# Destination rows of four blocks fetched from ScalarE's queue instead of by GpSimd's gather, in a graph attention layer

## The chip, the cores and the metric

One core of one Trainium2 chip runs the whole program. The number that counts is the device time of one execution in microseconds (us). The kernel before took 764.09 us, the median of 3 runs (762.74 to 765.07).

## The reference

A graph has 50,000 nodes with 64 features (`x`), and 25,000 edges, each with a source `src`, a destination `dst` (sorted), a 64-wide attribute and one of 10 types. With R = 10 relation matrices `Wr`:

```
proj   = x @ Wr                                  for every relation
t, h   = proj[src, type], proj[dst, type]
att    = sum(t * tanh(h + eattr))                per edge
a      = softmax of att over the edges of one destination
h_nb   = sum over edges of x[src] * a            per destination
out    = leaky((x + h_nb) @ W1.T) + leaky((x * h_nb) @ W2.T)
result = layernorm(x + out)                      per node
```

Most nodes have no edge. For them `h_nb` is 0, and the result needs `x` and `W1` alone.

## The kernel before, in words

**Two kinds of work run side by side.** The dense part treats every node as if it had no edge: 49 tiles of 1,024 nodes go through TensorE, ScalarE and VectorE and are stored to `out` in order. The edge part treats the edges as 128 partitions of T = 196 consecutive edges, cut into NS = 25 blocks `s` of 8 columns (the last one has 4). The rows of nodes that do have edges are then scattered over the dense rows of `out`. So no scatter may start before every dense row is stored.

**One loop over steps**, `for s in range(-1, NS + 4)`, stands on every engine, with the same `s`. In step `s` the engines do the relation products of block `s`, the softmax sums of block `s - 1`, the two output products of block `s - 2`, the layer norm of the blocks before that, and three dense tiles 3s+3, 3s+4, 3s+5 (D0, D1, D2), as long as there are any: the last tile, 48, is D0 of step 15. Each engine's program is a fixed order written by hand, and semaphores tie the engines together.

**Moving rows.** `xsd` is a ring of RX = 13 blocks; for each of the 8 columns of a block it holds 128 source rows (side 0) and 128 destination rows (side 1).

- POOL (GpSimd) runs one long queue: in `gather` one indirect DMA for each column and side, 384 in all, then in `scatter` one for each column, 196, with one extra gather (`es_end`) and one extra scatter at the end. Between the gathers and the scatters it waits for `o_stored`, that is for the last dense tile to have landed in `out`. `pace` makes POOL wait now and then for a mark of TensorE's progress, chosen by the number of moves made so far, so that it does not run far ahead.
- SP (SyncE) issues the plain loads and stores. It already fetches the last destination column of each of the 8 blocks in `ROW_BLOCKS` row by row (`rows_at`): it loads 8 row numbers from `row_ids` into registers and issues 8 DMAs of 256 bytes, up to six times in a step. These columns are left out of `columns(s)`, which is what `gather` walks. Before the loop, `load_ids(k)` brings the row numbers of those columns into `row_ids` by two DMAs each; VectorE multiplies them by the row size in step 0 (L1120).
- ScalarE (ACT) issues no DMA. Its program in a step is: `tanh`, `dense_copy(D0)`, `heads`, `dense_norm` of an older tile (`o_t`, eight activations), `dense_relu(D0)`, `weights` (waits for VectorE's `delta`), `weigh`, `dense_square`, `final_out`, `pair_copy` (`uwT`), `weigh`, `pair_copy`, `roots` (with two table loads), then in turn `pair_out` (`l`), `dense_copy` (`dT`), `dense_norm` (`o_t`), `dense_square` (`sqd`), `final_square` (`sqf`) and `dense_relu` (`rd`) for D1 and D2.

**Stores of the dense tiles.** In step `s` SP stores tile 2 of step `s - 2` and tiles 0 and 1 of step `s - 1` at fixed places between its row fetches: `load_typ`, `load_e`, `rows_at` (1), store, `load_x`, `rows_at` (2), `load_x`, `rows_at` (3), two stores, three more `rows_at`, `store_hist`. Tile 48 is therefore stored in step 16, behind the third `rows_at`.

Of the kernel before, what the change touches and what calls it, by code (L numbers as in the profile page):

```python
# [40 lines left out]
def gnn_resnorm(nc, x, src, dst, eattr, etype, relw, resw, resw2, out):  # L41
# [14 lines left out]
    def cols(s):  # L56
        return min(COLS, T - s * COLS)
# [24 lines left out]
    CHUNK = 8  # L82
    PER_STEP = 6

    def columns(s):
        return [(j, side) for side in range(2) for j in range(cols(s)) if not (s in ROW_BLOCKS and (j, side) == (cols(s) - 1, 1))]

# [8 lines left out]
    with ExitStack() as ctx:  # L96
# [38 lines left out]
        fix_i = sb("fix_i", [P, 2], I32)  # L135
        row_ids = sb("row_ids", [1, len(ROW_BLOCKS), P], I32)

# [51 lines left out]
        gathered = sems("gathered", RX)  # L189
        rows_in, ids_in = sems("rows_in", len(ROW_BLOCKS)), sem("ids_in")  # L190
        at_done = sem("at_done")
        typ_in = sems("typ_in", RT)
# [33 lines left out]
        def pe_marks():  # L226
# [56 lines left out]
            return marks, ends  # L283

        block = ctx.enter_context(nc.Block())

        @block.sync
        def _(sp):
# [64 lines left out]

            x_bytes = x.rearrange("n f -> (n f)").bitcast(U8)
            ROW = D * 4

            def load_ids(k):
                c = ROW_BLOCKS[k] * COLS + cols(ROW_BLOCKS[k]) - 1
                every = dst[0:(P - 1) * T].rearrange("(p c) -> c p", c=T)
                sp.dma_start(row_ids[0:1, k, 0:P - 1], every[c:c + 1, :], allow_slow_non_contiguous=True).then_inc(ids_in, DMA)  # L360
                last = (P - 1) * T + c if c < LASTC else c - LASTC
                sp.dma_start(row_ids[0:1, k, P - 1:P], dst[last:last + 1].rearrange("(a c) -> a c", a=1)).then_inc(ids_in, DMA)
# [26 lines left out]
            load_e(1)  # L389
            for k in range(len(ROW_BLOCKS)):  # L390
                load_ids(k)

# [97 lines left out]
        def _(pe):  # L490
# [12 lines left out]
            def turn_in(s):  # L503
                pe.wait_ge(gathered[s % RX], sum(len(columns(n)) for n in range(s % RX, s + 1, RX)) * DMA)
                if s in ROW_BLOCKS:
                    pe.wait_ge(rows_in[ROW_BLOCKS.index(s)], P * DMA)
                wait(pe, masked, s * R)
                half = cols(s) // 2
                for j in range(cols(s)):
                    k = j % 2 * half + j // 2  # L510
                    mm = pe.transpose(xT_ps[:, k * P:(k + 1) * P], xsd[:, s % RX, j, :, :].rearrange("p a f -> p (a f)"),
                                      ident[:, :])
                mm.then_inc(xT_done, 1)
# [147 lines left out]
        def _(act):  # L661
# [76 lines left out]
            def final_out(f, s):  # L738
# [5 lines left out]
                ins.then_inc(fmul_done, 1)  # L744

            act.wait_ge(setup_m, 2)
            for s in range(-1, LAST + 1):
# [9 lines left out]
                if D0 is not None:  # L757
                    dense_copy(D0)
                if 0 <= f < NS:
                    for g in range(groups(f)):  # L760
                        heads(f, g)
                for n in tiles(s - 2)[2:3]:
                    dense_norm(n)
                if D0 is not None:
                    dense_relu(D0)
                if 0 <= e < NS:
                    weights(e)
                    weigh(e, 0)
# [16 lines left out]
                for n in done[0:1]:  # L785
                    dense_norm(n)
                if quarters > 1:
                    pair_out(f, 1)
                if D0 is not None:
                    dense_square(D0)  # L790
                if 0 <= l < NS:
                    final_square(l)
                if D1 is not None:
                    dense_relu(D1)
                if quarters > 2:
                    pair_out(f, 2)
                if D2 is not None:
                    dense_copy(D2)
                for n in done[1:2]:
                    dense_norm(n)  # L800
                if quarters > 3:
                    pair_out(f, 3)
                if D1 is not None:
                    dense_square(D1)
                if s == NS + 1:

                    act.wait_ge(fx_v, 7)
                    act.activation(before[:, :], off[:, :], ACT.Exp, bias=fix[:, 5:6]).then_inc(fx_act, 1)
                    act.activation(fix[:, 6:7], fix[:, 2:3], ACT.Exp, bias=fix[:, 5:6]).then_inc(fx_act, 1)
# [18 lines left out]
        def _(v):  # L828
# [213 lines left out]
            for s in range(-1, LAST + 1):  # L1042
# [74 lines left out]
                if s == 0:  # L1117

                    v.wait_ge(ids_in, 2 * len(ROW_BLOCKS) * DMA)
                    v.tensor_scalar(row_ids[:, :, :], row_ids[:, :, :], float(4 * D), None, ALU.mult).then_inc(at_done, 1)  # L1120
# [92 lines left out]
```

## Time and profile before

| | us |
|---|---|
| median of 3 runs | 764.09 |
| span of the profiled execution (its own time; the page gives no more) | 764.9 |
| POOL busy | 581.8 (76%) |
| VectorE busy | 634.8 (83%) |
| PE busy | 556.2 (73%) |
| ScalarE busy | 499.1 (65%) |

A busy share counts only the instructions themselves. POOL shows 76%, but its digits in the slices of the span are 7 from the second slice to the last but one and never fall: each of its DMAs is followed by a short stretch called issue in which nothing is waited for. VectorE's digits are 9 until slice 34 and near 0 behind it; the last eighth of the span is scatters. The DMA engines are busy 40% or less of the time nearly everywhere.

### The profile page before, as it was taken

What the parts mean: (1) busy time and instruction counts of PE and PEld (TensorE: products, weight loads), DVE (VectorE), ACT (ScalarE), POOL (GpSimd) and SP (SyncE); (2) the same over time, 40 slices, a digit from 0 to 9 for tenths busy, and PEclk for the clock granted to TensorE, in tenths of its full rate; (3) what the DMA queues carried; (4) which work ended last, traced back from release to release, by engine and by line L of the source; (5) the groups of instructions that cost most, each with busy time, mean ns of one, the idle gap of its engine ahead of it and who ended that gap; (6) DMA issues with size and microseconds to landing.
All of it is one profiled execution on the core that took longest, in us unless ns stands there. A gap on an engine that the chain in (4) does not pass through costs nothing. (4 is left out here: it accounts for less than half of the span.)

```text
span 764.9 us, 14665 instructions
## 1 busy us (share of the span) xinstructions
PE 556.2 (73%) x3780; PEld 293.9 (38%) x3780; DVE 634.8 (83%) x1115; ACT 499.1 (65%) x1474; POOL 581.8 (76%) x590
## 2 busy tenths in 40 slices
PE   1887888888789788888889887788888788632000
PEld 0652454445345345345345343333333333321000
DVE  1689999999999999999999999999999899742010
ACT  0366677679778779779778777765656446755040
POOL 6777777777777777777777777777777777777776
PEclk9999999999999999999999999999999999755555
DMA  5463435434434434434444332422112221000000
GB/s 134 105 191 81 124 89 144 124 87 145 124 95 137 125 106 126 133 106 117 138 107 115 104 104 73 108 73 75 48 46 74 75 83 44 28 26 17 19 18 16
DMA packets 49457, 70.41 MB, mean 92 GB/s; under 512 B 17450, under 2 KB 20966, under 8 KB 49374
## 3 DMA queue, kind: packets, MB, share of 16 engines
q1 hardware_dynamic: 30750, 52.33, 21.2%
q0 software_dynamic: 18624, 17.16, 10.9%
q8 instruction: 30, 0.49, 0.3%
q14 instruction: 53, 0.43, 0.2%
HBM read 45.61 MB, written 25.78 MB: 93 GB/s over the span
## 5 line engine op out<-in xcount | busy, mean ns | idle before, releaser
L441 POOL DMA_INDIRECT xsd<-in_x,ends_i x384 | 378.2, 985 | 118.0 <-issue 108.6
L543 PE MATMUL t_ps<-xm,w_rel 64*64 64x512 f32 (+1 forms) x1000 | 270.3, 622 | 39.7 <-DVE xm L912 39.2
L912 DVE SCALAR_TENSOR_TENSOR xm<-typ,xT_ps 128x1024 f32<-128x1024 f32 (+1 forms) x250 | 292.4, 1187 | 2.6 <-issue 2.6
L545 PE MATMUL h_ps<-xm,w_rel 64*64 64x512 f32 (+1 forms) x1000 | 270.2, 622 | 0.0
L465 POOL DMA_INDIRECT out<-out_r,row_i x196 | 200.6, 1023 | 59.7 <-issue 55.5
L560 PE MATMUL y_ps<-bd_cat,dT 128*128 128x256 f32 x392 | 97.9, 394 | 17.6 <-DVE zd L974 14.8
L691 ACT ACTIVATE o_t<-zd,rstd 128x64 f32<-128x64 f32 x392 | 98.8, 337 | 14.9 <-DVE rstd L996 14.9
L543 PEld LDWEIGHTS t_ps<-xm,w_rel 64*64 64x64 f32 x1000 | 52.7, 135 | 142.7 <-DVE xm L912 117.4
L578 PE MATMUL s_ps<-bd_both,uwT 128*128 128x128 f32 x392 | 73.4, 313 | 36.6 <-issue 35.9
L578 PEld LDWEIGHTS s_ps<-bd_both,uwT 128*128 128x128 f32 x392 | 54.9, 203 | 115.1 <-issue 95.3
L560 PEld LDWEIGHTS y_ps<-bd_cat,dT 128*128 128x128 f32 x392 | 72.5, 195 | 30.9 <-issue 12.8
L954 DVE SCALAR_TENSOR_TENSOR es<-es,wd,wx 128x64 f32<-128x64 f32 x196 | 55.7, 284 | 11.7 <-ACT wx L704 0.6
L698 ACT ACTIVATE wd<-delta 128x16 f32<-128x16 f32 (+1 forms) x25 | 5.4, 216 | 88.7 <-DVE delta L942 84.4
L568 PE MATMUL tr_ps<-ident,uw 128*128 128x128 f32 x196 | 34.4, 302 | 27.0 <-ACT uwT L718 15.6
L723 ACT COPY l<-s_ps 128x256 f32<-128x256 f32 x98 | 35.2, 359 | 26.9 <-PE s_ps L578 26.9
L545 PEld LDWEIGHTS h_ps<-xm,w_rel 64*64 64x64 f32 x1000 | 52.7, 135 | 0.0
L704 ACT ACTIVATE wx<-xsd,wd 128x64 f32<-128x64 f32 x196 | 52.1, 337 | 0.8
L711 ACT ACTIVATE h_t<-es,rs 128x64 f32<-128x64 f32 x196 | 49.4, 337 | 0.0
L743 ACT ACTIVATE out_r<-zcf,rstd 128x64 f32<-128x64 f32 x196 | 49.2, 333 | 0.1
L568 PEld LDWEIGHTS tr_ps<-ident,uw 128*128 128x128 f32 x196 | 22.3, 150 | 66.8 <-issue 35.0
L974 DVE TENSOR_TENSOR zd<-rd,y_ps 128x512 f32<-128x512 f32 x49 | 33.4, 682 | 9.2 <-ACT rd L677 9.2
L684 ACT ACTIVATE sqd<-zd 128x512 f32<-128x512 f32 x49 | 30.9, 631 | 12.7 <-DVE zd L984 12.6
(143 smaller groups left out, 742.1 us busy)
## 6 DMA issues: line engine op xcount, KB each, us to landing
xsd<-in_x SPq DMA_DIRECT2D x1024, 0.2 KB
x_in<-in_x SPq DMA_DIRECT2D x48, 256.0 KB
typ<-typ_d SPq DMA_DIRECT2D x24, 512.0 KB
out<-o_t SPq DMA_DIRECT2D x48, 256.0 KB
xsd<-in_x,ends_i POOLq DMA_INDIRECT x384
hist<-es SPq DMA_DIRECT2D x24, 256.0 KB, 2.0
ea<-in_edge_attr SPq DMA_DIRECT2D x24, 224.0 KB
out<-out_r,row_i POOLq DMA_INDIRECT x196, 2.1
```

The lines of the kernel that those rows point to most:

```text
L441: pool.indirect_dma_start(xsd[:, s % RX, j, side, :], None, x[:, :], bass.IndirectOffsetOnAxis(ap=ends_i[:, side, c:c + 1], axis=0),).then ...
L465: pool.indirect_dma_start(out[:, :], bass.IndirectOffsetOnAxis(ap=row_i[:, c:c + 1], axis=0), out_r[:, s % RW, j, :], None, bounds_check=t ...
L543: pe.matmul(t_ps[h * D:(h + 1) * D, 0:n], w_rel[0:D, r, :], xm[0:D, b, h * n:(h + 1) * n], start=(r == 0), stop=(r == R - 1), skip_group_c ...
L545: mm = pe.matmul(h_ps[(1 - h) * D:(2 - h) * D, 0:n], w_rel[D:P, r, :], xm[D:P, b, (1 - h) * n:(2 - h) * n], start=False, stop=(r == R - 1) ...
L560: mm = pe.matmul(y_ps[:, j * 2 * P:(j + 1) * 2 * P], dT[:, d % 2, j * P:(j + 1) * P], bd_cat.rearrange("p k f -> p (k f)"), start=True, st ...
L568: mm = pe.transpose(tr_ps[:, j * P:(j + 1) * P], uw[:, g * QUAD + j, :, :].rearrange("p k f -> p (k f)"), ident[:, :])
L578: mm = pe.matmul(s_ps[:, YQ + j * P:YQ + (j + 1) * P], uwT[:, q // 2, k * P:(k + 1) * P], bd_both[:, :], start=True, stop=True)
L691: ins = act.activation(o_t[:, d % RO, j * D:(j + 1) * D], zd[:, d % RZ, j * D:(j + 1) * D], ACT.Copy, scale=rstd[:, s % 2, d % 3, j:j + 1])
L704: ins = act.activation(wx[:, j, :], xsd[:, e % RX, j, 0, :], ACT.Copy, scale=wd[:, e % 2, 0, j:j + 1])
L711: ins = act.activation(h_t[:, j, :], es[:, f % RS, j, :], ACT.Copy, scale=rs[:, f % 2, j:j + 1])
L912: v.scalar_tensor_tensor(xm[:, (s * R + r) % RM, 0:n], typ[:, s % RT, 0:n], float(r), xT_ps[:, 0:n], ALU.is_equal, ALU.mult).then_inc(mask ...
L954: v.scalar_tensor_tensor(es[:, e % RS, j, :], old, wd[:, e % 2, 1, j:j + 1], wx[:, j, :], ALU.mult, ALU.add).then_inc(chain_done, 1)
```

## The change

Besides the last destination column, the second last one of blocks 8, 13, 18 and 24 is now fetched row by row, from ScalarE's queue. POOL's gather leaves it out, so `columns` of these blocks is one shorter. `fetch(s, place)` stands at twelve places of ScalarE's step and issues two 256-byte DMAs at each, rows in order, from step 1 on until all 4 x 128 rows are out (step 22). Every 32 rows it first loads 32 row numbers into registers. TensorE waits for one more semaphore before it turns such a block. SP loads four more lists of row numbers before the loop. The row sizes and the definition of `x_bytes` only move.

```diff
     ROW_BLOCKS = list(range(5, 25, 3)) + [24]
+    ACT_BLOCKS = [8, 13, 18, 24]
+    ACT_CHUNK, ACT_STEP, ACT_AT_ONCE = 32, 24, 2
+
+    def fetched(s):
+        return [(cols(s) - 1, 1)] * (s in ROW_BLOCKS) + [(cols(s) - 2, 1)] * (s in ACT_BLOCKS)
     def columns(s):
-        return [(j, side) for side in range(2) for j in range(cols(s)) if not (s in ROW_BLOCKS and (j, side) == (cols(s) - 1, 1))]
+        return [(j, side) for side in range(2) for j in range(cols(s)) if (j, side) not in fetched(s)]
...
-            for k in range(len(ROW_BLOCKS)):
-                load_ids(k)
+            for k, b in enumerate(ROW_BLOCKS):
+                load_ids(k, b * COLS + cols(b) - 1)
+            for k, b in enumerate(ACT_BLOCKS):
+                load_ids(len(ROW_BLOCKS) + k, b * COLS + cols(b) - 2)
...
+                if s in ACT_BLOCKS:
+                    pe.wait_ge(act_rows_in[ACT_BLOCKS.index(s)], P * DMA)
...
+            def fetch(s, place):
+                for n in range((s - 1) * ACT_STEP + place * ACT_AT_ONCE, (s - 1) * ACT_STEP + (place + 1) * ACT_AT_ONCE):
+                    k, p = divmod(n, P)
+                    if s < 1 or k >= len(ACT_BLOCKS):
+                        return
+                    b = ACT_BLOCKS[k]
+                    if p == 0:
+                        act.wait_ge(at_done, 1)
+                        wait(act, z2_done, b - RX + 1)
+                    if p % ACT_CHUNK == 0:
+                        for i in range(ACT_CHUNK):
+                            ids[i] = act.alloc_register(f"act_id{n}_{i}")
+                        act.load([ids[i] for i in range(ACT_CHUNK)], row_ids[0:1, len(ROW_BLOCKS) + k, p:p + ACT_CHUNK])
+                    at = act.snap(ids[p % ACT_CHUNK], donate=True, min_val=0, max_val=(N - 1) * ROW)
+                    act.dma_start(xsd[p:p + 1, b % RX, cols(b) - 2, 1, :].bitcast(U8),
+                                  x_bytes[bass.DynSlice(at, ROW)].rearrange("(a c) -> a c", a=1)).then_inc(act_rows_in[k], DMA)
...
                 if quarters > 2:
                     pair_copy(f, 1)
+                fetch(s, 6)
                 if s >= 0:
                     roots(s)
...
-                    v.wait_ge(ids_in, 2 * len(ROW_BLOCKS) * DMA)
+                    v.wait_ge(ids_in, 2 * (len(ROW_BLOCKS) + len(ACT_BLOCKS)) * DMA)
```

ScalarE's order in the middle of a step, before. `uwT` is `pair_copy`, `wx` is `weigh`, `sd` and `fix` with their table loads are `roots`, `l` is `pair_out`:

```order
L718 COPY uwT<-tr_ps 128x512
L704 ACTIVATE wx<-xsd,wd 128x64 x4
L718 COPY uwT<-tr_ps 128x512
L730 ACT_TABLE_LOAD
L730 ACTIVATE sd<-ssq,eps_t 128x32
L731 ACT_TABLE_LOAD
```

The same place in the changed kernel (line numbers are those of the changed file):

```order
L727 COPY uwT<-tr_ps 128x512
L713 ACTIVATE wx<-xsd,wd 128x64 x4
L771 DMA xsd<-in_x 1x256 x2
L727 COPY uwT<-tr_ps 128x512
L771 DMA xsd<-in_x 1x256 x2
L739 ACT_TABLE_LOAD
L739 ACTIVATE sd<-ssq,eps_t 128x32
L740 ACT_TABLE_LOAD
```

Two row fetches (place 5) now stand between the second `wx` group and the second `uwT` copy, and two (place 6) between that copy and the first table load.

ScalarE's order in the last third of a step, before. `sqf` is `final_square`; `rd`, `dT`, `o_t` and `sqd` belong to the dense tiles D1 and D2:

```order
L736 ACTIVATE sqf<-zcf 128x512
L677 ACTIVATE rd<-y_ps 128x512
L723 COPY l<-s_ps 128x256
L672 COPY dT<-tr_ps 128x512
L691 ACTIVATE o_t<-zd,rstd 128x64 x8
L723 COPY l<-s_ps 128x256
L684 ACTIVATE sqd<-zd 128x512
```

The same place in the changed kernel, in a step in which the load of 32 row numbers falls on place 8:

```order
L745 ACTIVATE sqf<-zcf 128x512
L769 TENSOR_LOAD row_ids
L771 DMA xsd<-in_x 1x256 x2
L686 ACTIVATE rd<-y_ps 128x512
L732 COPY l<-s_ps 128x256
L681 COPY dT<-tr_ps 128x512
L771 DMA xsd<-in_x 1x256 x2
L700 ACTIVATE o_t<-zd,rstd 128x64 x8
L771 DMA xsd<-in_x 1x256 x2
L732 COPY l<-s_ps 128x256
L693 ACTIVATE sqd<-zd 128x512
```

The load and place 8 are new ahead of `rd`, place 9 ahead of the `o_t` group, and place 10 behind it.

SP's order at the end of the part ahead of the loop, before (`x_in` are dense tiles 4, 5 and 6):

```order
L360 DMA row_ids<-in_dst 1x127x1
L362 DMA row_ids<-in_dst 1x1
L305 DMA x_in<-in_x 128x512 x3
L330 DMA typ<-typ_d 128x1024
L344 DMA ea<-in_edge_attr 112x512
```

The same place in the changed kernel:

```order
L365 DMA row_ids<-in_dst 1x127x1
L367 DMA row_ids<-in_dst 1x1
L365 DMA row_ids<-in_dst 1x127x1
L367 DMA row_ids<-in_dst 1x1
L365 DMA row_ids<-in_dst 1x127x1
L367 DMA row_ids<-in_dst 1x1
L365 DMA row_ids<-in_dst 1x127x1
L367 DMA row_ids<-in_dst 1x1
L314 DMA x_in<-in_x 128x512 x3
L339 DMA typ<-typ_d 128x1024
L353 DMA ea<-in_edge_attr 112x512
```

Twelve pairs of such loads now stand ahead of the tiles where eight stood; everything behind them moves back by four pairs. On POOL the one row of gathers reads x380 instead of x384, and nothing else moves there.

## Rows read from the trace of the kernel before

**Rows 1.** The page's costliest groups: busy us, mean ns | idle before, releaser.
```profile
L441 POOL DMA_INDIRECT xsd<-in_x,ends_i x384 | 378.2, 985 | 118.0 <-issue 108.6
```
**Rows 2.** The chain that ended last, in order of time: start us, us, what.
```profile
759.15 0.97 POOL out L465
...
760.43 0.97 POOL out L482
```
**Rows 3.** Step 11: us, busy PE, PEld, DVE, ACT, POOL; clock, DMA share, GB/s.
```profile
337.80:366.00 28.20, 23.73 (x168) 13.09 (x164) 27.59 (x47) 22.89 (x70) 21.49 (x23) 1.00 0.41 119
```
**Rows 4.** Timeline of POOL where the gathers end: start us, us, instruction.
```profile
497.59 0.94 POOL L441 DMA_INDIRECT xsd<-in_x,ends_i  x1 [0.30 <-issue]
498.83 1.00 POOL L465 DMA_INDIRECT out<-out_r,row_i  x1 [0.30 <-issue]
```
**Rows 5.** Timeline of SP in steps 15 and 16.
```profile
467.22 3.21 SPq L311 DMA_DIRECT2D out<-o_t  x2
471.54 9.87 SPq L377 DMA_DIRECT2D xsd<-in_x  x24
...
494.35 0.73 SPq L311 DMA_DIRECT2D out<-o_t  x2
```
**Rows 6.** The page's DMA issues: KB each, median us to landing.
```profile
hist<-es SPq DMA_DIRECT2D x24, 256.0 KB, 2.0
```
**Rows 7.** Timeline of ScalarE: the norm of tile 48.
```profile
487.42 2.02 ACT L691 ACTIVATE o_t<-zd,rstd 128x64 f32<-128x64 f32 x8
```
**Rows 8.** SP's own waits: us in total, times, longest us.
```profile
SPq L311 <- ACT o_t L691: 43.6, 18, 4.3
```
**Rows 9.** All instructions on row_ids: ns min/median/max, first and last start us.
```profile
L374 SPq TENSOR_LOAD <-row_ids x128: 697/782/1088, 51.7 to 625.7; - x128
L360 SPq DMA_DIRECT2D row_ids<-in_dst x8: 583/597/702, 18.6 to 31.8; - x8
L362 SPq DMA_DIRECT2D row_ids<-in_dst x8: 937/1109/1982, 19.4 to 32.4; - x8
L1120 DVE TENSOR_SCALAR row_ids<-row_ids x1: 806/806/806, 48.8 to 48.8; 1x1024 int32<-1x1024 int32 x1
```
**Rows 10.** Timeline of SP: the first tiles behind the lists of row numbers.
```profile
33.58 1.30 SPq L305 DMA_DIRECT2D x_in<-in_x  x3
```
**Rows 11.** Timeline of PE in step 0: tile 4 is turned, then relation 6.
```profile
40.35 0.66 PE L553 MATMUL tr_ps<-ident,x_in 128*128 128x128 f32 x4
41.65 0.64 PE L543 MATMUL t_ps<-xm,w_rel 64*64 64x512 f32 x1 [0.64 <-DVE xm L912]
```
**Rows 12.** Timeline of SP: eight row fetches one behind the other.
```profile
302.65 2.60 SPq L377 DMA_DIRECT2D xsd<-in_x  x8
```
**Rows 13.** Timeline of ScalarE in step 10.
```profile
312.11 0.21 ACT L698 ACTIVATE wd<-delta 128x16 f32<-128x16 f32 x1 [2.89 <-DVE delta L942]
...
318.20 0.58 ACT L718 COPY uwT<-tr_ps 128x512 f32<-128x512 f32 x1 [0.30 <-issue]
...
322.85 2.02 ACT L691 ACTIVATE o_t<-zd,rstd 128x64 f32<-128x64 f32 x8 [0.17 <-DVE rstd L996]
...
326.08 0.58 ACT L677 ACTIVATE rd<-y_ps 128x512 f32<-128x512 f32 x1
...
326.88 0.58 ACT L672 COPY dT<-tr_ps 128x512 f32<-128x512 f32 x1
327.36 2.02 ACT L691 ACTIVATE o_t<-zd,rstd 128x64 f32<-128x64 f32 x8
329.29 0.35 ACT L723 COPY l<-s_ps 128x256 f32<-128x256 f32 x1
```
**Rows 14.** Timeline of VectorE in the same step.
```profile
324.41 0.71 DVE L1032 SCALAR_TENSOR_TENSOR zcf<-zs,zf 128x512 f32<-128x512 f32 x1
...
326.76 0.68 DVE L974 TENSOR_TENSOR zd<-rd,y_ps 128x512 f32<-128x512 f32 x1
...
329.79 1.17 DVE L1011 SCALAR_TENSOR_TENSOR l<-l 128x1024 f32<-128x1024 f32 x1
```

More of the change, by code:

```diff
@@ L135, in gnn_resnorm @@
         fix_i = sb("fix_i", [P, 2], I32)
-        row_ids = sb("row_ids", [1, len(ROW_BLOCKS), P], I32)
+        row_ids = sb("row_ids", [1, len(ROW_BLOCKS) + len(ACT_BLOCKS), P], I32)
         xsd = sb("xsd", [P, RX, COLS, 2, D])
@@ L190, in gnn_resnorm @@
         rows_in, ids_in = sems("rows_in", len(ROW_BLOCKS)), sem("ids_in")
+        act_rows_in = sems("act_rows_in", len(ACT_BLOCKS))
         at_done = sem("at_done")
@@ L283, in pe_marks @@
             return marks, ends
+        x_bytes = x.rearrange("n f -> (n f)").bitcast(U8)
+        ROW = D * 4
         block = ctx.enter_context(nc.Block())
@@ L352, in store_hist, with load_ids @@
                              es[:, e % RS, 0:cols(e), :]).then_inc(hist_stored[e % RS], DMA)
[L354 to L358, printed above, removed]
+            def load_ids(k, c):
                 every = dst[0:(P - 1) * T].rearrange("(p c) -> c p", c=T)
@@ L744, in final_out @@
                 ins.then_inc(fmul_done, 1)
+            ids = {}
+            def fetch(s, place):
[14 more added lines that the diff above has]
+                                  x_bytes[bass.DynSlice(at, ROW)].rearrange("(a c) -> a c", a=1)).then_inc(act_rows_in[k], DMA)
             act.wait_ge(setup_m, 2)
@@ L758, in _ @@
                     dense_copy(D0)
+                fetch(s, 0)
                 if 0 <= f < NS:
@@ L761, in _ @@
                         heads(f, g)
+                fetch(s, 1)
                 for n in tiles(s - 2)[2:3]:
                     dense_norm(n)
+                fetch(s, 2)
                 if D0 is not None:
@@ L768, in _ @@
                     weigh(e, 0)
+                fetch(s, 3)
                 if DP is not None:
@@ L772, in _ @@
                     final_out(o - 1, s - 1)
+                fetch(s, 4)
                 if quarters > 0:
@@ L776, in _ @@
                     weigh(e, 1)
+                fetch(s, 5)
                 if quarters > 2:
                     pair_copy(f, 1)
+                fetch(s, 6)
                 if s >= 0:
@@ L786, in _ @@
                     dense_norm(n)
+                fetch(s, 7)
                 if quarters > 1:
@@ L792, in _ @@
                     final_square(l)
+                fetch(s, 8)
                 if D1 is not None:
@@ L798, in _ @@
                     dense_copy(D2)
+                fetch(s, 9)
                 for n in done[1:2]:
                     dense_norm(n)
+                fetch(s, 10)
                 if quarters > 3:
@@ L804, in _ @@
                     dense_square(D1)
+                fetch(s, 11)
                 if s == NS + 1:
```

## The prediction, made before the changed kernel ran

> **What bounds the kernel now.** I read the slices of the page first, then the costliest groups, the chain of waits, the timeline of POOL where it changes from gathers to scatters, and the timeline of SP there. The slices show POOL equally busy from start to end. Its gather takes 0.985 us and stands behind 0.31 us of issue (118.0 / 384) [rows 1], 1.29 us a move, and the chain that ended last is scatters and nothing else [rows 2]. So POOL's queue sets the end, and a gather less is worth up to 1.29 us, if nothing else then holds POOL.
>
> Something stands ready to hold it. Before the first scatter POOL waits until the last dense tile, 48, has landed. The last gather starts at 497.59 and the first scatter at 498.83 [rows 4]. SP issues the two parts of tile 48 from 494.35 to 495.08 [rows 5]; a store of SP's lands 2.0 us after its issue [rows 6], so at 497.1, and with 0.3 us of issue the scatter could start at 497.4. The slack is 498.83 - 497.4 = 1.4 us. POOL may come earlier to this place, but it gets no more than 1.4 us out of it, as long as tile 48 is stored when it is now.
>
> Why is tile 48 stored so late? Its norm on ScalarE runs from 487.42 to 489.44 [rows 7], 4.9 us ahead of the store. SP is the late one: from its two stores of step 15, which end at 470.43 behind a wait for ScalarE, it works with small gaps up to 494.35 [rows 5]. That wait is the usual one: 43.6 us over 18 times, 2.4 us each [rows 8]. So SP follows the dense loop with 2.4 us to spare in a step, and tile 48's store comes a fixed 23.9 us behind the norm of tile 46 in step 15. Whatever delays the loop up to step 15 delays the first scatter by the same amount, less 1.4 us.
>
> The loop itself is bound by VectorE: 27.59 us of 28.20 in step 11, with ScalarE at 22.89 [rows 3]. ScalarE's spare 5.3 us lie mostly where it waits for `delta` (2.89 us at 312.11) [rows 13]. From the second `uwT` copy at 318.20 to the last `l` at 329.29 the rows leave no gap but 0.17 us.
>
> **The change, part by part.**
>
> *POOL.* Four gathers go: 4 x 1.29 = 5.2 us. The gathers then end near 493.3, and the wait for tile 48 is late next. By the slack above 1.4 us of the 5.2 remain, the rest becomes waiting. Pace marks only hold POOL if the loop slips, and by no more than it slips, which is late at the hand-over anyway; scatters further on stand behind results long finished, so no second gain or loss: every us at the hand-over is one at the end.
>
> *SP ahead of the loop.* Four more lists, each 0.60 + 1.11 us and two gaps of 0.05 [rows 9]: 4 x 1.75 = 7.0 us. The loads behind them are queued: tiles 4 to 6, types and edges of the next blocks. Tile 4 is issued by 34.0 (the first of three from 33.58 on [rows 10]) and, at 2.0 us to landing, is there at 36.0; with the change at 43.0. TensorE turns it at 40.35 [rows 11]: 2.65 us late. TensorE's own wait of 0.64 us behind it goes in return [rows 11], which leaves 2.0. TensorE is followed by the tanh and the product at the step's end, so the loop keeps this. Bounds 0 (it is swallowed later) and 2.7; I take 2.0. VectorE's multiplication of `row_ids` at 48.8 grows by half its 0.81 us [rows 9]; the lists are issued by about 40.6, so they are there. It lies in VectorE's wait for the tanh of step 0 and I cost it at nothing; without that cover 0.4.
>
> *ScalarE, the DMAs.* SP needs 0.325 us for each row fetch (2.60 / 8 [rows 12]), 0.65 for a pair, 7.8 for the 24 of a step. The trace shows no DMA on ScalarE. One bound is 0, when ScalarE works on activations handed to it earlier while the pair is issued; the other is all 7.8 exposed. I take cover where a group of eight activations (2.0 us) or a wait stands around the pair: places 0 to 5 (the 2.89 us at `delta` swallow what shows), 7, 8, 10 and 11. Two remain. Place 6 stands behind a copy that waits for TensorE (318.20, 0.58 us long [rows 13]); the pair ends at 318.85 plus the hand-over of the next waits, some 0.3 us late, less the 0.17 us idle ahead of `o_t`. Place 9 stands behind the `dT` copy at 326.88, so that the `o_t` group starts at about 327.6 in place of 327.36 [rows 13]. What waits for it: VectorE's `zd` at 326.76 needs `rd`, done at 326.66, and its `l` at 329.79 needs the copy done at 329.64 [rows 13, 14]: 0.1 and 0.15 us to spare. So about 0.25 us of a step shows on VectorE; over the 14 steps 1 to 14 that is 3.5 us (bounds 0 and, where the six places of that stretch show in full, 6 x 0.65 x 14 = 55).
>
> *ScalarE, the loads of row numbers.* 16 loads of 32 registers; SP's loads of 8 take 0.70 to 1.09 us, median 0.78 [rows 9]. Bounds 0.78 and 4 x 0.78 = 3.1; I take 1.1, nearer the row. With 24 rows in a step they fall on places 0, 4, 8 and none in turn. On 0 and 4 they are covered. On place 8, in steps 3, 7 and 11, the pair and the load take 1.75 us from the end of `zcf` at 325.12 [rows 14] on, which is 326.87, where `rd` started at 326.08: 0.8 late, 0.7 on VectorE, 0.6 beyond what is counted: 3 x 0.6 = 1.8.
>
> *SP beside ScalarE.* If the two queues get in each other's way, SP's last 23.9 us, in which it no longer waits, grow. Bounds 0 and 24 x 0.325 = 7.8; I take 1.0.
>
> *The new waits.* The rows of block 8 are out by step 6 and used at the end of step 7, those of 13, 18 and 24 by steps 11, 16 and 22 for 12, 17 and 23: a step of 28.20 [rows 3] covers the landing. `at_done` and `z2_done` are set by then. Cost nothing; if a block came late, TensorE and all behind it would wait.
>
> *Sum.* The loop slips 2.0 + 3.5 + 1.8 = 7.3 by the hand-over, SP adds 1.0: 8.3. Less 1.4 of slack: +6.9. The span of 764.9 becomes 771.8; the median stood 0.8 below the profiled span, so 771.0.
>
> **A page's rule beside the rows.** The trace shows ScalarE's eight-activation groups but not how far its queue is filled. The Trainium skill, "Advanced Engine Details and Errata", section Engine Queue Depths, gives ScalarE a queue of 8 on trn2: by that a pair issued behind a group of eight is hidden, as I assume. No row here tests it.
>
> **Rivals.**
>
> *All of ScalarE's issue is hidden, the hand-over holds.* For it: 5.3 us idle in a step. Against: the gapless stretch. The loop slips only by the 2.0 of the start, or not at all: 764.1 - 1.4 + 2.0 = 764.7, down to 762.7. No change. This is the case on the other side, not slower: the mechanism is POOL's shorter queue cut off at tile 48's landing, and it decides as soon as the loop and SP slip less than 1.4 + 2.3 = 3.7 us in all.
>
> *POOL gets its 5.2 us.* Only if tile 48 lands earlier or is not waited for; nothing in the rows makes SP earlier. 764.1 - 5.2 = 758.9.
>
> *ScalarE's issue is not hidden.* Its activations stand still while it issues: 22.89 + 7.8 + 0.8 of loads = 31.5 us against 28.20, 3.3 a step, 14 steps: 46, with start and slack about 811. ScalarE is then the bound.
>
> *SP and ScalarE share what issues the fetches.* SP has 2.4 us to spare in a step [rows 8]. If half of ScalarE's 7.8 us went on SP's queue, 1.5 a step would be lost, 21 over 14 steps, and 3.9 in the last stretch: 764.1 - 1.4 + 2.0 + 21 + 3.9 = 789.6. For it: SP is busy nearly without a gap. Against: a fetch is 256 bytes, and the two are often out of phase. The Trainium skill, "Perfetto Trace Analysis", section DMA Instruction — HWDGE, says that the unit which makes descriptors is shared between sequencers and locked while one uses it; by that such waits exist on both queues. The trace has one such queue only and cannot show it.
>
> **Chances.** The forecast, a slip that gives 767 to 782: 0.56. Hidden: 0.19. POOL's 5.2: 0.04. Not hidden: 0.11. Shared unit: 0.10. A difference under 0.3%, 2.3 us, can't be told from none here. Faster by more: 0.04. Within: 0.20, the hidden case and a sliver of the forecast. Slower: 0.76. The range 763.5 to 787 leaves out the fastest case with the lower end of the hidden one and most of the last two.
>
> **What would show it.** In the profile after: POOL's row has x380 gathers and an idle gap ahead of the first scatter, which starts near 506, with tile 48's store at about 503; the steps are 28.5 to 28.9 us long where they were 28.2; TensorE waits near 40 for tile 4. Wrong if the first scatter starts before 498, if the steps keep their length (then ScalarE's issue is free), or if ScalarE has no idle time left (then it is not hidden at all). SP's wait for ScalarE's `o_t` shrinking from 2.4 us each would point to the shared unit.

## The result, and the profile after

The changed kernel takes 782.09 us (median of 4 runs, 781.45 to 782.42); beside it the kernel before took 764.58 us (4 runs, 762.74 to 765.07). The ratio is 1.0226 (95% interval 1.0208 to 1.0243), 17.5 us slower. The forecast was 771.0, 6.9 us more than before: the direction was right, and the time lies in the range of 763.5 to 787.0, but the slip of the loop was more than twice what the sum gave.

The page of the kernel after, costliest groups (busy us, mean ns | idle before, releaser):

```profile
L448 POOL DMA_INDIRECT xsd<-in_x,ends_i x380 | 374.8, 986 | 125.2 <-issue 105.2
L1014 DVE TENSOR_TENSOR zd<-rd,y_ps 128x512 f32<-128x512 f32 x49 | 33.3, 680 | 19.5 <-ACT rd L686 19.4
```

Four gathers went at the old price each [rows 1]. VectorE's `zd` now waits 19.4 us for ScalarE's `rd`, where it waited 9.2 before. The timeline of POOL at the hand-over (start us, us, instruction, idle before it and its releaser):

```profile
501.43 0.94 POOL L448 DMA_INDIRECT xsd<-in_x,ends_i  x1 [0.30 <-issue]
515.75 1.00 POOL L472 DMA_INDIRECT out<-out_r,row_i  x1 [13.37 <-DMA out<-o_t]
```

The timeline of SP in steps 15 and 16:

```profile
482.33 6.36 SPq L320 DMA_DIRECT2D out<-o_t  x2
489.80 9.85 SPq L382 DMA_DIRECT2D xsd<-in_x  x24
...
512.51 0.73 SPq L320 DMA_DIRECT2D out<-o_t  x2
```

The first scatter starts 16.9 us later than before (515.75 against 498.83 [rows 4]) and stands behind 13.4 us of waiting for tile 48. From the end of SP's two stores of step 15 to the store of tile 48 it is 23.8 us, and 23.9 before [rows 5]. So SP's last stretch did not grow. All of the 16.9 us came with the loop.

Where the loop lost them is read from the first `xm` of a block on VectorE, the start of a step, once before and once after. Timeline of VectorE, kernel before, blocks 0, 1, 3, 4, 5 and 16:

```profile
31.81 2.34 DVE L912 SCALAR_TENSOR_TENSOR xm<-typ,xT_ps 128x1024 f32<-128x1024 f32 x2
...
55.50 1.21 DVE L912 SCALAR_TENSOR_TENSOR xm<-typ,xT_ps 128x1024 f32<-128x1024 f32 x1
...
108.89 1.21 DVE L912 SCALAR_TENSOR_TENSOR xm<-typ,xT_ps 128x1024 f32<-128x1024 f32 x1
137.08 1.21 DVE L912 SCALAR_TENSOR_TENSOR xm<-typ,xT_ps 128x1024 f32<-128x1024 f32 x1
165.26 1.21 DVE L912 SCALAR_TENSOR_TENSOR xm<-typ,xT_ps 128x1024 f32<-128x1024 f32 x1
...
473.99 1.21 DVE L912 SCALAR_TENSOR_TENSOR xm<-typ,xT_ps 128x1024 f32<-128x1024 f32 x1
```

The same of the kernel after:

```profile
32.20 1.21 DVE L952 SCALAR_TENSOR_TENSOR xm<-typ,xT_ps 128x1024 f32<-128x1024 f32 x1
...
60.00 1.20 DVE L952 SCALAR_TENSOR_TENSOR xm<-typ,xT_ps 128x1024 f32<-128x1024 f32 x1
...
114.39 1.21 DVE L952 SCALAR_TENSOR_TENSOR xm<-typ,xT_ps 128x1024 f32<-128x1024 f32 x1
145.99 1.21 DVE L952 SCALAR_TENSOR_TENSOR xm<-typ,xT_ps 128x1024 f32<-128x1024 f32 x1
174.23 1.21 DVE L952 SCALAR_TENSOR_TENSOR xm<-typ,xT_ps 128x1024 f32<-128x1024 f32 x1
...
492.24 1.21 DVE L952 SCALAR_TENSOR_TENSOR xm<-typ,xT_ps 128x1024 f32<-128x1024 f32 x1
```

The differences are 0.4, 4.5, 5.5, 8.9, 9.0 and 18.3 us. Step 0 lost 4.1 us, step 3 lost 3.4, step 4 nearly nothing. Over all steps up to block 16, from the same kind of row:

| lost in | us |
|---|---|
| start and step 0 (lists of row numbers) | 0.4 + 4.1 |
| steps 3, 7, 11, 15 (load on place 8) | 3.4 + 2.1 + 2.2 + 3.0 = 10.7 |
| steps 2, 6, 10, 14 (load on place 4) | 1.0 + 0.5 + 0.3 + 0.8 = 2.6 |
| all others (load on place 0, or none) | 0.5 |
| sum | 18.3 |

18.3 less the slack of 1.4 is the 16.9 at the hand-over. Steps with 24 fetches and no load on places 4 or 8 cost next to nothing. A load of 32 row numbers is the first row here, a fetch on ScalarE's and on SP's queue are the others (ns min/median/max):

```profile
L769 ACTq TENSOR_LOAD <-row_ids x16: 2132/2144/2542, 56.3 to 599.4; - x16
...
L771 ACTq DMA_DIRECT2D xsd<-in_x x512: 213/213/537, 58.6 to 628.6; - x171
...
L382 SPq DMA_DIRECT2D xsd<-in_x x1024: 227/228/347, 57.0 to 648.1; - x171
```

The forecast took 1.1 us for the load. It is 2.14. The timeline of ScalarE and VectorE in step 3, kernel after:

```profile
132.83 0.62 ACT L745 ACTIVATE sqf<-zcf 128x512 f32<-128x512 f32 x1
...
134.66 0.75 ACTq L771 DMA_DIRECT2D xsd<-in_x  x2
...
135.51 0.60 ACT L686 ACTIVATE rd<-y_ps 128x512 f32<-128x512 f32 x1 [2.06 <-issue]
...
136.14 0.69 DVE L1014 TENSOR_TENSOR zd<-rd,y_ps 128x512 f32<-128x512 f32 x1 [2.02 <-ACT rd L686]
```

The load ends where the pair begins, so it began at about 132.4. Only `sqf` was left to ScalarE meanwhile. `rd` starts 2.06 us after `sqf` is done, and VectorE, the bound of the loop, stands still for 2.02 of them. Before, the two stood without a gap; this is ScalarE in the same place of the kernel before:

```profile
127.34 0.62 ACT L736 ACTIVATE sqf<-zcf 128x512 f32<-128x512 f32 x1
127.86 0.58 ACT L677 ACTIVATE rd<-y_ps 128x512 f32<-128x512 f32 x1
```

And the start. TensorE turns tile 4 and goes on with a relation (timeline of PE, kernel after):

```profile
44.02 0.66 PE L562 MATMUL tr_ps<-ident,x_in 128*128 128x128 f32 x4 [3.21 <-DMA x_in<-in_x]
44.61 1.09 PE L552 MATMUL t_ps<-xm,w_rel 64*64 64x512 f32 x1
```

It waits 3.2 us for the tile, and the matmuls behind the wait take 1.09 us instead of 0.64 [rows 11]. The granted clock in that stretch is 0.58 (first row, after); before it was 1.00 (second row; us, busy PE, PEld, DVE, ACT, POOL, clock, DMA share, GB/s):

```profile
44.00:48.00 4.00, 3.98 (x16) 1.93 (x17) 2.78 (x3) 3.02 (x10) 3.08 (x4) 0.58 0.90 263
```
```profile
44.00:48.00 4.00, 3.78 (x26) 1.56 (x25) 3.68 (x5) 4.00 (x15) 2.91 (x4) 1.00 0.33 90
```

Of the two levels, 2.4 GHz is 1.00 and 1.2 GHz is 0.50, so a mean of 0.58 is the lower level for most of the stretch. TensorE had been idle for 3.2 us ahead of it.

### The profile page after: what moved, and what is told of

It is laid out like the page before. It is cut to its first block and busy times, and to the rows that moved or that the text cites. A ratio compares the mean times of both kernels' runs of the same rounds, so it can differ in the third digit from the quotient of the medians.

```text
span 780.7 us, 15717 instructions
## 1 busy us (share of the span) xinstructions
PE 560.1 (72%) x3780; PEld 295.0 (38%) x3780; DVE 636.2 (81%) x1115; ACT 502.0 (64%) x1474; POOL 577.4 (74%) x586
## 3 DMA queue, kind: packets, MB, share of 16 engines
q10 hardware_dynamic: 1024, 0.13, 0.1%
## 5 line engine op out<-in xcount | busy, mean ns | idle before, releaser
L552 PE MATMUL t_ps<-xm,w_rel 64*64 64x512 f32 (+1 forms) x1000 | 273.3, 627 | 35.8 <-DVE xm L952 35.1
L554 PE MATMUL h_ps<-xm,w_rel 64*64 64x512 f32 (+1 forms) x1000 | 273.3, 627 | 0.0
L569 PE MATMUL y_ps<-bd_cat,dT 128*128 128x256 f32 x392 | 98.9, 397 | 16.9 <-DVE zd L1014 14.2
L700 ACT ACTIVATE o_t<-zd,rstd 128x64 f32<-128x64 f32 x392 | 98.8, 337 | 14.9 <-DVE rstd L1036 10.4
L994 DVE SCALAR_TENSOR_TENSOR es<-es,wd,wx 128x64 f32<-128x64 f32 x196 | 55.7, 284 | 11.7 <-ACT wx L713 0.6
L1014 DVE TENSOR_TENSOR zd<-rd,y_ps 128x512 f32<-128x512 f32 x49 | 33.3, 680 | 19.5 <-ACT rd L686 19.4
L1051 DVE SCALAR_TENSOR_TENSOR l<-l 128x1024 f32<-128x1024 f32 (+1 forms) x25 | 29.7, 1190 | 13.9 <-ACT l L732 13.7
```

Of the source, the lines that this page charges most:

```text
L552: pe.matmul(t_ps[h * D:(h + 1) * D, 0:n], w_rel[0:D, r, :], xm[0:D, b, h * n:(h + 1) * n], start=(r == 0), stop=(r == R - 1), skip_group_c ...
L554: mm = pe.matmul(h_ps[(1 - h) * D:(2 - h) * D, 0:n], w_rel[D:P, r, :], xm[D:P, b, (1 - h) * n:(2 - h) * n], start=False, stop=(r == R - 1) ...
L569: mm = pe.matmul(y_ps[:, j * 2 * P:(j + 1) * 2 * P], dT[:, d % 2, j * P:(j + 1) * P], bd_cat.rearrange("p k f -> p (k f)"), start=True, st ...
L700: ins = act.activation(o_t[:, d % RO, j * D:(j + 1) * D], zd[:, d % RZ, j * D:(j + 1) * D], ACT.Copy, scale=rstd[:, s % 2, d % 3, j:j + 1])
L994: v.scalar_tensor_tensor(es[:, e % RS, j, :], old, wd[:, e % 2, 1, j:j + 1], wx[:, j, :], ALU.mult, ALU.add).then_inc(chain_done, 1)
```

## The experiments

Theory C: the scatters start when tile 48 has landed, the loop's slip passes through less 1.4 us, and the slip is made of the lists and of loads that stick out of ScalarE's cover. Theory D (and other letters where named): another part carries it. Ratios are to the kernel before, timed on the same chip: 763.81 us for the first four, 764.96 for the next four, 765.21 for the last two.

**1. The gathers gone, nothing in their place.**

```diff
-        return [... if not (s in ROW_BLOCKS and (j, side) == (cols(s) - 1, 1))]
+        left_out = [(cols(s) - 1, 1)] * (s in ROW_BLOCKS) + [(cols(s) - 2, 1)] * (s in [13, 16, 19, 22])
+        return [... if (j, side) not in left_out]
```

> The kernel before with four gathers fewer and nothing in their place: the second last destination column of blocks 13, 16, 19 and 22 is left out, so those blocks compute with the rows that their ring slot held before. Nothing else differs. Theory A (the hand-over from gathers to scatters waits for tile 48's landing): the four gathers are worth 4 x 1.29 = 5.2 us of POOL's queue, but only 1.4 us come through: 764.6 - 1.4 = 763.2, no measurable change, and in the profile an idle gap of about 4 us on POOL ahead of the first scatter that ends with the landing of out<-o_t. Rival B (POOL's queue alone sets the end): 764.6 - 5.2 = 759.4, and no gap.

Measured: 763.58 us, ratio 0.9997 (0.9985 to 1.0009). POOL's waits (us in total, times, longest):

```profile
POOL out L466 <- DMA out<-o_t: 5.3, 1, 5.3
```

Four gathers are worth nothing that can be told while tile 48 is stored where it is: POOL turns them into waiting. That is A. The 1.4 us that A lets through don't show in the time either (0.2 us, and the interval reaches from 1.1 less to 0.7 more).

**2. The same, with the store of tile 48 earlier.** In step 16 it stands ahead of SP's second group of row fetches, where it stood behind the third.

```diff
+                last = tiles(s - 1)[0:1] == [ND - 1]
+                if last:
+                    store_o(ND - 1)
                 rows_at((s - 1) * PER_STEP + 1)
                 load_x(d + 5)
                 rows_at((s - 1) * PER_STEP + 2)
-                for n in tiles(s - 1)[0:2]:
+                for n in [] if last else tiles(s - 1)[0:2]:
```

> As e1_no_fetch (the same four columns are left out), and in step 16 SP issues the store of tile 48 ahead of its second row fetch group instead of behind its third. Its norm is done at 489.4, so the store can go out at 489.5 to 490.2 and land near 492.2, ahead of POOL's last gather (493.3). Theory A: now all of the 5.2 us come through, 759.4, and the gap on POOL is gone. If something else than the landing of tile 48 held POOL in e1_no_fetch, this changes nothing against it.

Measured: 760.69 us, ratio 0.9955 (0.9940 to 0.9970). The first scatter, in the timeline of POOL:

```profile
494.30 1.53 POOL L469 DMA_INDIRECT out<-out_r,row_i  x1 [3.36 <-DMA out<-o_t]
```

It starts 4.5 us earlier than before, and the kernel is 3.1 us faster than the one before, 2.9 faster than experiment 1: the landing of tile 48 sets the end, and SP's place for its store sets the landing. The full 5.2 us did not come through (759.4 was expected), and POOL still waits 3.4 us. Part of this is that the loop of the profiled execution was already 2.2 us late at its first block and 1.2 late at block 16, for a reason that was not looked into.

**3. Only the four lists more.** The kernel before with `load_ids` for twelve columns instead of eight; all 384 gathers stay.

```diff
-            for k in range(len(ROW_BLOCKS)):
-                load_ids(k)
+            for k, b in enumerate(ROW_BLOCKS):
+                load_ids(k, b * COLS + cols(b) - 1)
+            for k, b in enumerate([8, 13, 18, 24]):
+                load_ids(len(ROW_BLOCKS) + k, b * COLS + cols(b) - 2)
```

> The kernel before with four more lists of row numbers ahead of the loop (12 pairs of loads on SP, not 8), which nobody uses; all 384 gathers stay. The changed kernel's step 1 starts 4.1 us later than before, as TensorE waits 3.2 us for tile 4 and then multiplies at half speed for a while. Theory A: step 1 again starts about 4.1 us late, the slip is kept until the hand-over, and of it 4.1 - 1.4 = 2.7 us show in the time: 767.3. Rival: the slip is swallowed by later steps, or POOL does not depend on it: 764.6 within 1 us. My forecast had priced the slip at 2.0, which would give 765.2.

Measured: 766.49 us, ratio 1.0031 (1.0018 to 1.0044), 2.7 us. Timeline of PE, and the granted clock of the stretch behind it (0.59, the third number from the end):

```profile
43.06 0.66 PE L554 MATMUL tr_ps<-ident,x_in 128*128 128x128 f32 x4 [2.67 <-DMA x_in<-in_x]
```
```profile
44.00:48.00 4.00, 4.00 (x16) 2.09 (x8) 2.35 (x3) 2.77 (x10) 2.89 (x4) 0.59 0.95 257
```

The same wait, the same lower clock. The loop is 3.4 us late at block 1 and 2.8 at block 16. That is A.

**4. Only the loads.** The changed kernel, but POOL gathers all 384 columns and ScalarE issues one DMA of 64 bytes behind each load, where the other 31 fetches are left out.

```diff
-        return [(cols(s) - 1, 1)] * (s in ROW_BLOCKS) + [(cols(s) - 2, 1)] * (s in ACT_BLOCKS)
+        return [(cols(s) - 1, 1)] * (s in ROW_BLOCKS)
...
-                    act.dma_start(xsd[p:p + 1, b % RX, cols(b) - 2, 1, :].bitcast(U8),
-                                  x_bytes[bass.DynSlice(at, ROW)]...
+                        act.dma_start(spare[0:1, q, :].bitcast(U8),
+                                      x_bytes[bass.DynSlice(at, 64)]...
```

> The changed kernel without its row fetches on ScalarE: POOL gathers all 384 columns again, ScalarE still makes its 16 loads of 32 registers at the same places and, so that the registers are used, one 64-byte DMA behind each load. The four lists stay. Theory C (the loads, 2.14 us each where I had taken 1.1, are what the forecast missed): step starts slip by 4.1 us at step 0, by about 2.5 us in each of steps 3, 7, 11 and 15, by some 0.5 in steps 2, 6, 10 and 14, nothing elsewhere: 4.1 + 10 + 2 = 16 at the hand-over, less 1.4: 764.6 + 14.6 = 779. Rival D (the fetches themselves take the time, and the loads only happen to stand near): the slip stays near 4.1 + 2 and the time near 769.

Measured: 775.76 us, ratio 1.0165 (1.0141 to 1.0189), 12.0 us. It lies between the two expectations, nearer to C, which had a slip of 16 us at block 16 where it is 12.2. Without the lists of experiment 3 it is 9.3 us for 16 loads. The four steps with a load on place 8 lose 1.8, 1.5, 1.9 and 2.4 us. `rd` in step 3 (timeline of ScalarE):

```profile
133.83 0.60 ACT L687 ACTIVATE rd<-y_ps 128x512 f32<-128x512 f32 x1 [1.73 <-issue]
```

**5. Only the DMAs.** All 512 fetches stand where they are; the row numbers are loaded once, in step 1, and used again, so that the rows fetched are not the right ones.

```diff
-                    if p % ACT_CHUNK == 0:
+                    if n == 0:
```

> The changed kernel with its 512 row fetches at the same places, but with the row numbers loaded once (32 registers in step 1) and used again for all of them: the fetched rows are the wrong ones, the traffic is the same. The loads alone made the loop slip by 8.5 us (e4_loads_only against e3_lists_only), the whole change by 14 beyond the lists. Theory C (the fetches are covered by ScalarE's queued activations and cost only where they stand behind a load that has used the cover up): the slip is that of the lists, 3.4 to 4.1 us, plus at most 2; the time 764.6 + 5 - 1.4 = 768, and the step starts move nowhere by more than 0.5 us. Rival E (loads and fetches add up): slip 4 + 6 = 10, 773.

Measured: 768.69 us, ratio 1.0049 (1.0033 to 1.0065), 3.7 us, of which the lists are 2.7. About 1 us is left for 512 fetches, no more than the intervals. The steps agree: from block 1 to block 16 the loop loses 1.2 us. Timeline of ScalarE at place 8:

```profile
327.54 0.22 ACTq L771 DMA_DIRECT2D xsd<-in_x  x1
327.80 0.62 ACT L745 ACTIVATE sqf<-zcf 128x512 f32<-128x512 f32 x1
327.92 0.22 ACTq L771 DMA_DIRECT2D xsd<-in_x  x1
328.32 0.58 ACT L686 ACTIVATE rd<-y_ps 128x512 f32<-128x512 f32 x1
```

The pair is issued while `sqf` stands handed over behind `sqd` (327.27 to 327.90) and while it runs, and `rd` follows without a gap. ScalarE's DMAs are hidden behind activations already handed over. That is C.

**6. The lists later.** The changed kernel, with the four lists behind tile 7's load in step 0 instead of ahead of the loop.

```diff
-            for k, b in enumerate(ACT_BLOCKS):
-                load_ids(len(ROW_BLOCKS) + k, b * COLS + cols(b) - 2)
...
                 load_x(d + 4)
+                if s == 0:
+                    for k, b in enumerate(ACT_BLOCKS):
+                        load_ids(len(ROW_BLOCKS) + k, b * COLS + cols(b) - 2)
```

> The changed kernel with its four lists of row numbers loaded in step 0, behind the load of tile 7, where they delay no tile that is waited for. Theory A: TensorE no longer waits for tile 4, step 1 starts within 0.5 us of before, and the slip at the hand-over goes from 18.3 to about 14.2: 782.1 - 4.1 = 778. Rival: the later steps swallow it, 782.

Measured: 776.66 us, ratio 1.0152 (1.0121 to 1.0184). It stands 11.7 us above the kernel before, where the changed kernel stands 17.5 above it: 5.8 us less. Block 1 starts 0.3 us ahead of the kernel before, where it stood 4.5 behind; block 16 is 12.4 us late, where it was 18.3.

**7. The loads at place 0.** The changed kernel, with the 24 row numbers of a step loaded at its first place: 22 loads instead of 16, and none on place 4 or 8.

```diff
-                    if p % ACT_CHUNK == 0:
-                        for i in range(ACT_CHUNK):
+                    if n % ACT_STEP == 0:
+                        count = min(ACT_STEP, len(ACT_BLOCKS) * P - n)
+                        for i in range(count):
                             ids[i] = act.alloc_register(f"act_id{n}_{i}")
```

> The changed kernel with 24 row numbers loaded at place 0 of every step (22 loads, about 0.22 + 24 x 0.06 = 1.7 us each) in place of 32 at places 0, 4 and 8 in turn. 22 loads take more of ScalarE's time in all than 16 (37 against 34 us), but place 0 stands ahead of ScalarE's long wait for delta. Theory C (what counts is where a load stands): slip 4.1 from the lists plus at most 2, time near 768; no jump in steps 3, 7, 11 and 15. Rival D (what counts is the time that loads and fetches take on ScalarE's queue in all): no better than 782.

Measured: 766.95 us, ratio 1.0030 (1.0013 to 1.0047). The instructions (ns min/median/max) and ScalarE's waits (us in total, times, longest):

```profile
L771 ACTq TENSOR_LOAD <-row_ids x22: 742/1664/2074, 55.0 to 602.6; - x22
```
```profile
ACT wd L707 <- DVE delta L984: 43.3, 23, 6.2
ACT h_t L720 <- issue: 39.8, 20, 2.3
```

That is 2.0 us above the kernel before instead of 17.5, with the same 512 numbers and six loads more. ScalarE still stands 2 us ahead of `heads` for each load, 39.8 us in all, but its wait for `delta` further on shrinks by as much: 84.4 us in the kernel before (below), 43.3 here. A load at place 0 is paid out of that wait.

```profile
ACT wd L698 <- DVE delta L942: 84.4, 24, 6.4
```

**8. All three edits.** The changed kernel with the edits of experiments 6, 7 and 2. Part of its edit; the rest is shown there:

```diff
-    ACT_CHUNK, ACT_STEP, ACT_AT_ONCE = 32, 24, 2
+    ACT_STEP, ACT_AT_ONCE = 24, 2
...
+                if s == 0:
+                    for k, b in enumerate(ACT_BLOCKS):
+                        load_ids(len(ROW_BLOCKS) + k, b * COLS + cols(b) - 2)
+                last = tiles(s - 1)[0:1] == [ND - 1]
+                if last:
+                    store_o(ND - 1)
```

> Lists late, loads at place 0 of every step, and the store of tile 48 ahead of SP's second row fetch group in step 16; otherwise the changed kernel. Theory: slip at the hand-over 2 us or less, tile 48 stored at about 491.5 and landed at 494, first scatter near 495 to 496 where it was 498.8: 764.6 - 3 = 761.6, faster than both kernels. If the slip is 5 us or more, no faster than before.

Measured: 762.19 us, ratio 0.9963 (0.9945 to 0.9980): faster than the kernel before by 2.8 us, where the changed kernel is slower by 17.5. The hand-over (timeline of POOL):

```profile
493.23 0.94 POOL L452 DMA_INDIRECT xsd<-in_x,ends_i  x1 [0.30 <-issue]
494.48 1.00 POOL L476 DMA_INDIRECT out<-out_r,row_i  x1 [0.30 <-issue]
```

POOL no longer waits there, and the first scatter starts 4.35 us earlier than in the kernel before.

**9. The same without the earlier store.** Against experiment 8:

```diff
-                last = tiles(s - 1)[0:1] == [ND - 1]
-                if last:
-                    store_o(ND - 1)
...
-                for n in [] if last else tiles(s - 1)[0:2]:
+                for n in tiles(s - 1)[0:2]:
```

> The changed kernel with the four lists loaded behind tile 7's load in step 0 and with each step's 24 row numbers loaded at place 0, as in the kernel with all three edits, but with tile 48 stored at its old place in SP's step. Theory C (the scatters start when tile 48 has landed; what moved the loop is gone with the lists and with the load on place 8): the loop slips by no more than 1 us, POOL waits some 4 us for tile 48 and gives back of its 5.2 us only the 1.5 of slack: 764.0 to 764.5 against 765 before, no difference that can be told. Rival (the earlier store is not what made the kernel with all three faster): 762.2 again.

Measured: 764.90 us, ratio 0.9989 (0.9976 to 1.0002). The waits of POOL:

```profile
POOL out L473 <- DMA out<-o_t: 4.7, 1, 4.7
```

The gathers taken from POOL turn into waiting again. The intervals of experiments 8 and 9 just touch, so the traces decide: the first scatter starts at 498.14 here and at 494.48 there. With experiments 1 and 2, where the times alone tell them apart, it is the store's place that makes a shorter queue worth anything.

**10. Loads of 8.** The changed kernel with 64 short loads, on places 0, 4 and 8 of every step.

```diff
-    ACT_CHUNK, ACT_STEP, ACT_AT_ONCE = 32, 24, 2
+    ACT_CHUNK, ACT_STEP, ACT_AT_ONCE = 8, 24, 2
```

> The changed kernel with 64 loads of 8 row numbers in place of 16 of 32. They fall on places 0, 4 and 8 of every step. Each is taken as long as SP's, 0.78 us. Theory C (a load costs what sticks out of ScalarE's spare time at its place): at place 8 about 1.0 us lie free between the end of zcf and the start of rd; load and pair take 0.8 + 0.5 + small gaps = 1.4 us, so some 0.4 us of each of 14 steps sticks out, 5.6 us, and the lists cost their 3 to 4: slip 9 to 10, less 1.5: 772.5. Theory D (a load always costs its length, wherever it stands): 42 loads up to the hand-over x 0.78 = 33 us, with the lists 36: about 799. Theory E (only the long loads stick out): the lists alone, 767 to 768.

Measured: 778.65 us, ratio 1.0180 (1.0159 to 1.0201), 13.4 us. No expectation fits; C is nearest, too low by 6. The mechanism is C's and the size again is not. ScalarE at place 8 (the instructions, and the timeline):

```profile
L769 ACTq TENSOR_LOAD <-row_ids x64: 717/722/1132, 53.5 to 613.5; - x64
```
```profile
304.46 0.62 ACT L745 ACTIVATE sqf<-zcf 128x512 f32<-128x512 f32 x1
304.88 0.75 ACTq L771 DMA_DIRECT2D xsd<-in_x  x2
305.73 0.60 ACT L686 ACTIVATE rd<-y_ps 128x512 f32<-128x512 f32 x1 [0.66 <-issue]
```

`rd` is 0.66 us late with a load of 0.72, 2.06 late with a load of 2.14, and 0 without one. From the load of 8 to the load of 32 the lateness grows by 1.40 us and the load by 1.42. The pair alone uses up the cover of `sqf`, and a load on place 8 then shows in full. The steps here lose 0.3 to 1.3 us each (10.4 from block 1 to block 16), in place of the 0.4 expected. The profiled execution was the shortest of five. In it TensorE waited 1.98 us for tile 4 and kept its clock, so it lost 1.1 us in step 0 where the changed kernel lost 4.1.

## Why the prediction was right in kind and wrong in size

*POOL, right.* Every us at the hand-over is one at the end: +16.9 there, +15.8 in the span (780.7 against 764.9). From the first scatter to the end it is 263.7 to 266.4 us in all twelve profiles. The slack was forecast at 1.4 us, and 18.3 of slip gave 16.9; in the nine profiles of changed kernels with the store at its old place the first scatter moves by the slip at block 16 less 1.0 to 1.4 us. The time rose by 17.5 us, 1.7 more than the span. The traced execution of the kernel before was not among the timed ones: wherever a time and a span belong to one execution the time is 1.7 to 2.5 us longer, so the traced one took some 2 us more than the median of 764.58. Experiments 1, 2 and 9 show that the wait for tile 48 takes all else that POOL saves.

*The loads of row numbers, the step that failed.* "Bounds 0.78 and 4 x 0.78 = 3.1; I take 1.1, nearer the row", for three steps on place 8, was to cost 1.8 us. Three things were wrong. The load took 2.14 us. The working itself holds: with 2.14 in place of 1.1 its 0.8 us of lateness becomes 1.84, and the trace shows 2.06. The loads on place 8 fall in steps 3, 7, 11 and 15, not three but four: step 15 was outside the 14 steps counted, but its last third runs ahead of tile 48's norm. And those on place 4, called covered, cost 2.6 us. There `uwT` stands idle for 2.63 us in step 2:

```profile
91.63 0.63 ACT L693 ACTIVATE sqd<-zd 128x512 f32<-128x512 f32 x1 [0.49 <-DVE zd L1024]
...
94.89 0.59 ACT L727 COPY uwT<-tr_ps 128x512 f32<-128x512 f32 x1 [2.63 <-issue]
```

In all 13.3 us of slip stand where 1.8 were forecast. Four times 2.06 are 8.2 of the 10.7 on place 8. Steps 3 and 15 lost more than one such gap (3.4 and 3.0), and the traces show where. In step 3 TensorE, which had stood idle for 1.84 us up to 136.5, ran at the lower level in 136.8 to 140.3 (granted clock 0.51, first row). Its eight `y_ps` took 3.42 us, where the same eight took 1.95 in experiment 6 at a granted clock of 1.00. ScalarE's next `rd` waited 1.05 us for them, and VectorE 1.21 us for the `g_t` behind that `rd` (second row). Experiment 6 has no such wait and loses 2.2 us in this step.

```profile
136.80:140.30 3.50, 3.50 (x12) 2.71 (x10) 3.40 (x7) 2.75 (x11) 2.89 (x3) 0.51 0.20 61
```
```profile
142.28 0.69 DVE L959 TENSOR_TENSOR prod<-t_ps,g_t 128x512 f32<-128x512 f32 x1 [1.21 <-ACT g_t L676]
```

In step 15 there are no D1 and D2 any more, so no `rd` follows place 8, and the load delays ScalarE's `l` copies instead. VectorE's `l` waits 3.75 us for them (first row) where it waited 0.72 before (second row): 3.0 us, all that the step lost.

```profile
488.58 1.23 DVE L1051 SCALAR_TENSOR_TENSOR l<-l 128x1024 f32<-128x1024 f32 x1 [3.75 <-ACT l L732]
```
```profile
470.32 1.23 DVE L1011 SCALAR_TENSOR_TENSOR l<-l 128x1024 f32<-128x1024 f32 x1 [0.72 <-ACT l L723]
```

Loads and fetches cost more together than apart: lists 2.7, loads 9.3 and fetches 1.0 add up to 13.0 of the 17.5 us. The traces show where the missing 4.5 are: on place 8 the steps lose 10.7 us with the fetches and 7.6 with one DMA behind each load, on place 4 2.6 and about 1.3.

*The lists, half right.* The forecast of 2.0 us rested on TensorE waiting 2.65 us for tile 4. Its four lists of 0.60 + 1.11 us and two gaps of 0.05 come to 7.2 us and not to 7.0, and tile 4 was issued 6.8 us later (40.39 against 33.58 [rows 10]); but it landed near 44.0 and not at 43.0. TensorE waited 3.2 us and the step lost 4.1, since the matmuls behind the wait ran at the lower clock. That second part was missing. Its size varies: of two executions with equal waits of 2.6 us, experiment 5 kept its clock and lost 1.8, which is near the forecast for such a wait, and experiment 7 did not (0.67 in the same stretch) and lost 3.3. Experiment 6 shows 5.8 us in the time for the place of the lists, and 5.8 less slip at block 16: 4.8 of it at block 1, and 1.2 in step 3, where the lower clock described above is absent.

*ScalarE's DMAs, wrong the other way.* 3.5 us were forecast for places 6 and 9, and about 1 is left in experiment 5. The rows of experiment 5 show the cover at place 8, and the prediction's own sign, steps that keep their length, came out in the steps without a load on place 4 or 8. The Trainium skill, "Advanced Engine Details and Errata", section Engine Queue Depths, gives ScalarE a queue of 8. The trace agrees that DMAs are issued beside queued activations, but the queue is not full where the loads stand. In step 2 the load began at 91.6, together with the `sqd` ahead of it, for which ScalarE had waited 0.49 us (row above). In step 3 it began at 132.4, when VectorE's `zcf`, which `sqf` waits for, was done (131.68 + 0.71), with the end of `sqd` and `sqf` as all its cover. So the load seems not to start before the activation ahead of it is released; no run tests that by itself.

*SP beside ScalarE, nothing.* 1.0 us was forecast and the last stretch is 23.8 for 23.9. A fetch takes 228 ns on SP in both kernels (in the kernel before 225/228/323 ns), and SP's wait for `o_t` grew instead of shrinking: 61.1 us over 19 times against 43.6 over 18 [rows 8]. So the shared unit of the fourth rival shows in no run.

```profile
SPq L320 <- ACT o_t L700: 61.1, 19, 5.8
```

*Sum.* In the order lists, ScalarE's DMAs, loads, SP, slack the forecast was 2.0 + 3.5 + 1.8 + 1.0 - 1.4 = 6.9. The steps of the changed kernel give 4.5 + 0.5 + 13.3 + 0 - 1.4 = 16.9, where the 0.5 is what all steps without a load on place 4 or 8 lost.

*Rivals.* "All hidden" was right on the DMAs and wrong on the loads: experiment 9, in which all stands under cover, took 0.3 us less than the kernel before (765.21 on that chip), where the rival gave 1.4 less to 0.6 more. "POOL gets its 5.2" needs tile 48 to land earlier, as it said, and experiment 8 has 4.35 of them. The case that ScalarE's issue is not hidden (811) is far off.

## What to carry to other kernels

An engine that works from a queue hides what its sequencer (the part that issues its DMAs and register loads, ACTq in the rows) does only as long as handed-over work lasts: look at what is queued behind the last wait, not at the engine's idle share, and put a long sequencer instruction ahead of the place where the engine waits anyway (place 0 here: 15.5 us). Scale an unseen instruction by its count of elements before taking a value "nearer the row", and count the steps up to the instruction that is waited for, not up to the last whole one. Before shortening a queue, move what it will wait for next: with the loads and lists out of the way the shorter queue saved nothing that can be told (experiment 9) until the store of tile 48 stood earlier (experiment 8). The store moved alone, with all 384 gathers, was not run.

## What the runs showed of the hardware

- Loading registers on ScalarE took 0.722 us for 8, 1.66 for 24 and 2.14 for 32 (medians): 0.059 us for each register and 0.25 beside it. The Trainium skill, "DMA: Bandwidth & Descriptors", section Latency and other measured facts, gives such a load a floor of about 600 ns, and the 0.72 of eight, the shortest here, lies above it. "Runtime: NRT & Kernel Launch", section Instruction fetch mechanics, of the same Trainium skill, gives about 200 ns for each register, for loads that the page describes as coming from HBM. By that 32 would take an estimated 6.4 us, three times what the trace shows for a load from `row_ids`.
- TensorE waited 2.6 to 3.2 us for tile 4 in five of the profiled executions. In four the granted clock from 44.0 to 48.0 was low: 0.58 in the changed kernel, 0.59, 0.57 and 0.67 in experiments 3, 4 and 7. In experiment 5, after 2.62 us, it was full, as it was in experiment 10 after 1.98 us. Experiment 5:

```profile
44.00:48.00 4.00, 4.00 (x26) 1.90 (x21) 3.08 (x4) 3.45 (x11) 3.08 (x4) 1.00 0.84 269
```

- A fetch of 256 bytes took 213 ns on ScalarE's queue and 228 ns on SP's (medians). SP's 1,024 took the same 228 ns with ScalarE's 512 beside them as without; ScalarE's were never run without SP's.
